# Head 0 of the first cross attention: keys loaded straight into the stacked layout and split there, the queries scaled tile by tile

## The reference

```python
q = qkv.reshape(bs * N_HEADS, ch, length)
k = v = y.reshape(bs * N_HEADS, ch, -1)
weight = jnp.einsum('bct,bcs->bts', q * scale, k * scale)
weight = jax.nn.softmax(weight.astype(jnp.float32), axis=-1)
a = jnp.einsum('bts,bcs->bct', weight, v)
...
x = x + _L0_xattn_ref(_layernorm(x, axis=-1), ctx_2048)
```

## Time and profile before

| what | value |
|---|---|
| median of 3 runs | 1378.21 us (1376.22 to 1380.72) |
| time of the profiled execution | 1381.22 us |
| its span | 1379.4 us |
| PE busy | 1337.7 us, 97% |
| DVE busy | 1098.2 us, 80% |
| ACT busy | 970.9 us, 70% |
| POOL busy | 156.3 us, 11% |
| DMA | 199.51 MB, mean 145 GB/s |

### The profile page before, as it was taken

One profiled execution on the slowest core, in us unless ns is written; L12 is line 12 of the kernel. 1 busy time (PEld: TensorE's weight loads), 2 busy tenths in 40 slices (PEclk: granted clock), 3 DMA queues, 4 the chain that ended last, 5 costly groups with the idle time before them and its releaser, 6 DMA issues. The chain is left out here.

```text
span 1379.4 us, 28331 instructions
## 1 busy us (share of the span) xinstructions
PE 1337.7 (97%) x10623; PEld 883.2 (64%) x10623; DVE 1098.2 (80%) x2195; ACT 970.9 (70%) x1892; POOL 156.3 (11%) x216
## 2 busy tenths in 40 slices
PE   3999999999999999999999999999999999999999
PEld 2544444444444444444457999999988874668998
DVE  5889989899999999997876766666668759887665
ACT  1499999999999999999574555555544631785553
POOL 4122221122222222112000000000000000000000
PEclk9899999999999999999999999999999999999999
DMA  7555566565665555555303755555529614204651
GB/s 189 124 143 116 126 173 166 154 164 110 142 143 127 115 135 131 121 96 79 100 1 139 305 184 186 184 187 186 190 94 373 244 68 177 69 1 129 183 190 39
DMA packets 75338, 199.51 MB, mean 145 GB/s; under 512 B 35512, under 2 KB 43616, under 8 KB 63040
## 3 DMA queue, kind: packets, MB, share of 16 engines
q1 hardware_dynamic: 75024, 197.69, 50.7%
q10 hardware_dynamic: 192, 0.20, 0.1%
HBM read 170.64 MB, written 23.80 MB: 141 GB/s over the span
## 5 line engine op out<-in xcount | busy, mean ns | idle before, releaser
L754 ACT ACTIVATE probs<-bank 128x512 f32<-128x512 f32 x1024 | 542.1, 619 | 54.3 <-PE bank L812 52.0
L672 DVE TENSOR_REDUCE pm<-bank 128x1 f32<-128x512 f32 x736 | 466.1, 682 | 51.2 <-PE bank L793 50.9
L812 PE MATMUL bank<-qst,kst 52*128 52x512 f32 (+1 forms) x1024 | 336.6, 437 | 7.8 <-DMA qst<-nscratch 7.1
L793 PE MATMUL bank<-kst,qst 48*128 48x512 f32 x904 | 315.6, 452 | 21.4 <-DMA qst<-qsplit 20.3
L824 PE MATMUL bank<-probs,vext 128*32 128x256 f32 (+3 forms) x4024 | 295.1, 394 | 0.8
L812 PEld LDWEIGHTS bank<-qst,kst 52*128 52x128 f32 (+1 forms) x1024 | 163.6, 187 | 197.3 <-DVE pm L672 93.6
L1602 PE MATMUL bank<-e_xhi,e_hi 128*128 128x256 f32 (+1 forms) x768 | 217.6, 283 | 0.3 <-DVE e_xlo L283 0.2
L1602 PE MATMUL bank<-e_xhi,e_lo 128*128 128x256 f32 (+1 forms) x768 | 217.5, 283 | 0.0
L1602 PE MATMUL bank<-e_xlo,e_hi 128*128 128x256 f32 (+1 forms) x768 | 217.5, 283 | 0.0
L824 PEld LDWEIGHTS bank<-probs,vext 128*32 128x32 f32 x4024 | 92.6, 109 | 117.8 <-issue 103.9
L793 PEld LDWEIGHTS bank<-kst,qst 48*128 48x128 f32 x904 | 140.5, 189 | 30.5 <-DMA qst<-qsplit 20.3
(11 more groups left out here) (251 smaller groups left out, 1763.8 us busy)
## 6 DMA issues: line engine op xcount, KB each, us to landing
raw<-wall SPq DMA_DIRECT2D x43, 1536.0 KB, 6.6
kst<-kscratch SPq DMA_DIRECT2D x192, 128.0 KB, 4.4
kscratch<-ksplit SPq DMA_DIRECT2D x15, 1024.0 KB, 4.3
kraw<-ctx_rows SPq DMA_DIRECT2D x16, 512.0 KB, 6.2
vraw<-ctx_vt SPq DMA_DIRECT2D x16, 512.0 KB, 6.3
ctxT<-ctxT SPq DMA_DIRECT2D x8, 1024.0 KB, 9.7
nat<-ctx_chunks SPq DMA_DIRECT2D x6, 1024.0 KB, 19.9
weights<-wscratch SPq DMA_DIRECT2D x16, 256.0 KB, 3.8
```

Source lines behind the costliest of these rows:

```text
L672: nc.vector.tensor_reduce(max_at(p, 1), bank[:, pre_bank(p), :], AX.X, ALU.max).then_inc(pre_reduced, 1)
L754: nc.scalar.activation(probs[:, (XST * k + n) % PR, :], bank[:, score_bank(XST * k + n), :], ACT.Exp, scale=XSCALE).then_inc(probs_ready, 1)
L793: ins = nc.tensor.matmul(bank[:, pre_bank(p), :], qst[64 * j:64 * j + KR, h, tt * P:tt * P + P], keys, start=True, stop=True)
L812: nc.tensor.matmul(bank[:, score_bank(s), :], kst[64 * j:64 * j + rows, h % 2, m * P:m * P + P], qst[64 * j:64 * j + rows, h, :], start=Tr ...
```

## The change

Head 0's keys are no longer rounded, stored and loaded again. SP loads them raw, straight into the stacked layout: `load_first(half)` issues eight transfers of 16 partitions x 2048 numbers, the four groups of 16 rows in both partition halves, into `first_raw`. A column `low_row` holds 1 on the rows of the low part and 0 elsewhere. One multiplication writes `first_high` (rounded keys on the low rows, zero elsewhere) and one subtraction writes `kst`: key minus rounded key on the low rows, the rounded key on the others. DVE does this for the first half, POOL for the second (`second_keys`). The second half's loads wait for the first half's and for the queries in `qst`.

The token tiles are loaded and normalised apart: tile 0 first, on DVE; tile 1's statistics follow on DVE behind the keys, and its scaling and splitting go to POOL (`second_queries`). The memsets of `marks` go to the front of POOL's list, and POOL now runs `second_keys()`, `split(1)`, `split_apart(1)`, `second_queries()` in this order. `load_q` waits for its own tile only. The loads of head 1's raw keys and pairs stand behind `load_first(1)`.

```diff
+FIRST_LOADS = 8 * 16
+FIRST_KEYS = [1, 3]
+SECOND_SCALED = 14
...
+            def load_first(half):
+
+                keys = ctx_rows[0].rearrange("(c s) n -> c (s n)", c=XC)
+                for row in range(0, 64, XC):
+                    for j in range(2):
+                        lo = j * XK + half * XK // 2
+                        sp.dma_start(first_raw[64 * j + row:64 * j + row + XC, half, :], keys[:, lo:lo + XK // 2]).then_inc(kraw_loaded[0], 16)
+
-            sp.dma_start(X[:, :, :], x.rearrange("(a p) d -> p a d", p=P)).then_inc(x_loaded, 16)
-            load_raw(0)
+            sp.dma_start(X[:, 0, :], x[0:P]).then_inc(x_loaded[0], 16)
+            load_first(0)
+            sp.dma_start(X[:, 1, :], x[P:]).then_inc(x_loaded[1], 16)
+            sp.wait_ge(kraw_loaded[0], FIRST_LOADS)
+            sp.wait_ge(stack_lo[0], 96)
+            load_first(1)
             load_raw(1)
             load_pairs(1)
-            sp.wait_ge(split_step, 1)
-            sp.dma_start(kscratch[0, 0], ksplit[:, 0, :].bitcast(F32)).then_inc(first_high_stored, 16)
-            sp.wait_ge(split_step, 2)
-            sp.dma_start(kscratch[0, 1], ksplit[:, 1, :].bitcast(F32)).then_inc(split_stored, 16)
-            sp.wait_ge(first_high_stored, 16)
-            load_rows(0, 0, K_ROWS[0])
-            load_rows(0, 0, K_ROWS[2])
-            sp.wait_ge(split_stored, 16)
-            load_rows(0, 0, K_ROWS[1])
-            sp.wait_ge(stack_lo[0], 192)
-            load_stack(0, 1)
-            sp.wait_ge(qsplit_ready, 4)
...
+            def second_keys():
+
+                pool.wait_ge(kraw_loaded[0], FIRST_LOADS * 2)
+                pool.wait_ge(split_step, FIRST_KEYS[0])
+                nc.gpsimd.tensor_scalar(first_high[:, 1, :], first_raw[:, 1, :], low_row[:, :], None, ALU.mult).then_inc(split_step, 1)
+                pool.wait_ge(split_step, FIRST_KEYS[0] + 1)
+                nc.gpsimd.tensor_tensor(kst[:, 0, XK // 2:], first_raw[:, 1, :], first_high[:, 1, :].bitcast(F32),
+                                        ALU.subtract).then_inc(split_step, 1)
...
+            second_keys()
+            split(1)
+            split_apart(1)
+            second_queries()
...
+            dve.wait_ge(kraw_loaded[0], FIRST_LOADS)
+            link(nc.vector.tensor_scalar(first_high[:, 0, :], first_raw[:, 0, :], low_row[:, :], None, ALU.mult))
+            nc.vector.tensor_tensor(kst[:, 0, 0:XK // 2], first_raw[:, 0, :], first_high[:, 0, :].bitcast(F32),
+                                    ALU.subtract).then_inc(split_step, 1)
+            dve.wait_ge(x_loaded[1], 16)
+            tile_spread(g, 0, 1, link)
+            tile_small(g, dve, 0, 1, link)
...
-                    pe.wait_ge([stack_lo, stack_hi][half][h % 2], stacked(h, half))
+                    if h == 0:
+                        pe.wait_ge(split_step, FIRST_KEYS[half])
+                    if k != 1:
+                        pe.wait_ge([stack_lo, stack_hi][half][h % 2], stacked(h, half))
```

More of the change, by code:

```diff
@@ L88, in raw_loads @@
 def raw_loads(h):
[L89 removed]
+    return 80 * (h // 2 + h % 2) + FIRST_LOADS * NS * (1 - h % 2)
 def cuts(h):
[L93 removed]
+    return 5 * h
 def stacked(h, half):
[L97 removed]
+    return [192, 96][half] * (h // 2 + 1) + 48 * (h // 2 + h % 2) - 96 * (1 - h % 2)
 def score_bank(s):
@@ L189, in setup @@
     return g
[L193 to L215, removed]
 def roots(k, a):
-    return TA * k + a
+    return TA * k + a + 1
 def turned_bank(k, a):
@@ L436, in load_stack @@
                 if half == 0:
-                    sp.wait_ge(split_stored, 32 * h + 16)
+                    sp.wait_ge(split_stored, 32 * h)
                 if h >= 2:
@@ L587, in values @@
                 nc.gpsimd.tensor_copy(vext[:, h % 2, :, 0:XC], vraw[:, h % 2]).then_inc(v_ready, 1)
-            split(0)
-            pool.wait_ge(qsplit_ready, 4)
-            split(1)
-            split_apart(1)
+            def second_keys():
[5 more added lines that the diff above has]
+                                        ALU.subtract).then_inc(split_step, 1)
             nc.gpsimd.memset(marks[:, :, :].bitcast(F32), 1.0).then_inc(const_set, 1)
@@ L631, in _ @@
                 if h == XH - 1:
-                    pool.wait_ge(split_stored, 32 * XH - 16)
+                    pool.wait_ge(split_stored, 32 * (XH - 1))
                     pool.wait_ge(nsplit_step, 2 * NS * h + 2)
@@ L649, in link @@
                 dve.wait_ge(dve_step.sem, dve_step.inc(ins))
-            dve.wait_ge(x_loaded, 16)
-            norm_dve(g, dve, link)
-            for a in range(TA):
-                dve.wait_ge(g.xn_ready, a + 1)
-                nc.vector.tensor_copy(qsplit[:, 0, a], xn[:, a, :]).then_inc(qsplit_ready, 1)
-                dve.wait_ge(qsplit_ready, 2 * a + 1)
-                nc.vector.tensor_tensor(qsplit[:, 1, a], xn[:, a, :], qsplit[:, 0, a].bitcast(F32), ALU.subtract).then_inc(qsplit_ready, 1)
+            dve.wait_ge(g.ident_ready, 2)
+            link(nc.vector.tensor_reduce(low_row[:, :], ident[:, :].rearrange("p (j r c) -> p r j c", j=2, c=XC)[:, 1], AX.XY, ALU.add))
+            dve.wait_ge(x_loaded[0], 16)
+            tile_spread(g, 0, 0, link)
+            tile_scale(g, dve, 0, 0, link)
+            dve.wait_ge(g.xn_ready, 1)
+            nc.vector.tensor_copy(qsplit[:, 0, 0], xn[:, 0, :]).then_inc(qsplit_ready, 1)
+            dve.wait_ge(qsplit_ready, 1)
+            nc.vector.tensor_tensor(qsplit[:, 1, 0], xn[:, 0, :], qsplit[:, 0, 0].bitcast(F32), ALU.subtract).then_inc(qsplit_ready, 1)
+            dve.wait_ge(kraw_loaded[0], FIRST_LOADS)
[5 more added lines that the diff above has]
+            tile_small(g, dve, 0, 1, link)
+            link(nc.vector.scalar_tensor_tensor(out=g.rstd[:, 1, :], in0=g.std[:, 1, :], scalar=1.5, in1=g.rstd[:, 1, :],
+                                                op0=ALU.add, op1=ALU.mult))
             def turn_negmax(k):
@@ L739, in _ @@
             nc.scalar.activation(g.warm[:, :], ident[:, 0:1], ACT.Sqrt)
-            act.wait_ge(kraw_loaded[0], 16)
-            nc.scalar.copy(ksplit[:, 0, :], kraw[:, 0, :]).then_inc(split_step, 1)
-            act.wait_ge(g.var_ready, 1)
-            nc.scalar.activation(g.std[:, :, :], g.var[:, :, :], ACT.Sqrt).then_inc(g.std_ready, 1)
+            tile_root(g, act, 0, 0)
             for row, part in Q_ROWS:
```

31 lines of the change are left out of this document (23 added, 8 removed).

## The result

| | before | after |
|---|---|---|
| median | 1378.18 us (4 runs, 1376.22 to 1380.72) | 1391.88 us (4 runs, 1391.21 to 1392.72) |
| profiled execution and its span | 1381.22, 1379.4 us | 1391.84, 1390.0 us |

The ratio is 1.0091, with a 95% interval of 1.0070 to 1.0111: the change makes the kernel slower by 13.7 us on the medians. The whole interval lies outside the 0.3% that count as no change. Three of 21 later executions of the kernel before took 1385.5 to 1387.6 us, so medians are compared here and not single executions.

What follows compares the result with a forecast made beforehand. The first real score, held by SP's queue behind POOL's split of head 1, bounds the start: 33.1 + 5.7 + 12.5 = 51.3, score 4.9 later at 56.2, +8.4 us; 1378.2 + 8.4 = 1386.6 us, range 1379.0 to 1393.6.

Steps and rivals of the forecast that it cites:

- Only the start counts, and the first score carries it: Whole kernel: PE is busy after the start, so the change is worth the first real score's shift, 47.77 to 56.2 us.
- PE's start: First pre product at 15.5 us: direct loads landed at 12.0, then DVE's multiplication 1.2 and subtraction 2.3; first pair 17.8.
- The rival of slower loads: Direct loads of head 0's keys at 117 GB/s, 2.1 us more per half: +4.2, 1390.8 us; chance 0.12.
- The head start is eaten by the queue: First pair 3.4 us earlier, but SP's queue delays the score; the rival that it reaches the end: 1374.8 us, chance 0.09.
- POOL's multiplication, 1.9 us between 1.8 and 4.7: POOL multiplies 2048 columns of head 0's second half: 1.9 us, sized from a memset, a copy and a two-input instruction.
- Head 1's keys stored at 33.1: SP's store of head 1's keys at 33.1 us instead of 23.05, since POOL's split(1) stands behind head 0's second half.
- 5.7 us from the store to the key loads: SP's queue from the store of head 1's keys to the key loads, marks included: 5.7 us, before 7.27.
- 12.5 us from the key loads to the store of the maxima: SP's queue from first key load to the store of the maxima: 12.5 us carried over, so stored at 51.3.
- The queue would not stall on the marks (0.18): Rival on SP's queue: key loads take 2.7 us, the score comes at 50.2, +2.4, 1380.6 us; chance 0.18.
- The clock, no term: PE's low clock after restart loses 3.7 us as before, so no term; twice as long, 1390.3 us, had chance 0.06.
- DVE idle until about 41.5 for POOL's split maxima: DVE waits for POOL's split_negmax(0) until about 41.5 us; its seven pairs end at 50, before the score, so free.
- The score ended by the maxima's loads: Sign in the profile: the first score near 56 us, its wait ended by the maxima loaded into qst.

Runs made afterwards that it cites:

- e1: Changed kernel with the multiplication of the second half of head 0's keys moved from POOL to ACT: 1388.12 us, ratio 1.0065.
- e4: Changed kernel with head 1's raw keys and pairs loaded, and POOL's split of head 1 run, ahead of head 0's second half: 1389.51 us, ratio 1.0077.
- e5: Changed kernel with two of the four copies of marks, those for head 1's buffer, issued on ACT's queue: 1389.89 us, ratio 1.0087.
- e8: Changed kernel with the edits of e4 and e1, POOL's second_keys behind queries and memsets, and marks behind head 1's stacked-key and query loads: 1379.81 us, ratio 1.0010.
- e9: As e8, with the two copies of marks for head 1's buffer on ACT's queue behind its multiplication: 1380.58 us, ratio 1.0017.
- e10: As e8, with only head 0's two copies of marks ahead of the first maxima and head 1's two behind the first score's inputs: 1375.28 us, ratio 0.9983.
- e11: Changed kernel with only head 1's two copies of marks moved behind the first score's inputs: 1386.75 us, ratio 1.0070.
- e2: Kernel before, with SP holding the store of head 1's keys until 13 pairs of pre tiles are reduced: 1391.92 us, ratio 1.0095.
- e3: Changed kernel with PE's first pre product held until the second half of head 0's raw keys has landed: 1394.11 us, ratio 1.0111.
- e12: Kernel before, with head 1's two copies of marks moved behind the first score's inputs: 1378.33 us, ratio 0.9992.
- e7: Changed kernel with 30 more filling products on PE behind the last pre product: 1389.22 us, ratio 1.0084.
- e6: Changed kernel with POOL's multiplication by the constant 1.0 instead of low_row, which makes the second half's keys wrong: 1392.04 us, one run.

## Why the prediction was right, and where not

The forecast was 1386.6 us in 1379.0 to 1393.6, slower with a chance of 0.73. The kernel is slower, at 1391.88; the median lies in the range, 5.3 us above the forecast. By its steps:

- **Only the start counts, and the first score carries it.** Right. The shift of the score and of the median against before are +13.4 and +13.7 us; in e1 +10.0 and +9.9, in e4 +10.0 and +11.3, in e5 +12.4 and +11.7, in e8 +2.7 and +1.6, in e9 +2.4 and +2.4, in e10 -1.8 and -2.9, in e11 +9.7 and +8.6, in e2 +13.3 and +13.7, in e3 +14.7 and +15.9, in e12 -0.9 and +0.2. They agree within 1.4 us. e7 is the exception (+14.8 and +11.0), with its shorter stretch of low clock.
- **PE's start.** 15.5 predicted, 14.58 measured, just below the 15 to 16.5 that were to show it; first pair 17.8 and 16.59. The eight direct loads were issued from 1.20 and had landed at 10.92. The sum let them start at 4.1 and take 6.9 us at 152 GB/s; they had landed 6.8 us after 4.1, and from 4.1 to 10.9 the engines moved 164 GB/s, token tile 1 and the queries included. The second half landed 9.4 us after its first issue, where the sum has 9.2 (of these, 1.4 and 0.9 us stand there without a row). The rival of slower loads fell. The Trainium skill, page "SBUF — State Buffer", section "Door 1: The DMA port swizzle", gives 104 GB/s for a transfer to 16 partitions at 1 MiB; with several such transfers in flight, to different rows, the engines moved about half more here.
- **The head start is eaten by the queue.** Right. It is now 4.6 us and changes nothing of the score; e3 gave up 8.1 us of it and lost 2.2 at most.
- **POOL's multiplication, 1.9 us between 1.8 and 4.7.** Wrong: 5.45 us, above the upper bound. This is the first failed step, +3.55 us. I had put it beside a memset and a copy because it has one input; the rows say that it costs more than the subtraction of the same size with two inputs (4.62, predicted 4.6). The Trainium skill, page "GPSIMD Engine Reference", section "Engine selection", calls operations with one input roughly line-rate; the trace agrees for the copy of 1024 in 1.04 us, 1.0 ns for a column, and disagrees for TENSOR_SCALAR, 2.7 ns for a column.
- **Head 1's keys stored at 33.1.** 35.95: 3.55 late by the multiplication, 0.8 early by the landing at 22.3 instead of 23.1.
- **5.7 us from the store to the key loads.** Wrong: 9.1 us (35.95 to 45.04), 3.4 more, of which the marks are 3.0: the four took 5.96 us to issue and not 2.99. This is the second failed step; I had carried the row over as it stood, though I took the marks to be slow. Before, the queue took all four, and the hold fell on a key load behind them (a single issue of 4.12 us); now it falls on the third and the fourth mark already, and the key loads are the shorter for it: 7.51 instead of 8.75. Why the queue took four at once before, and only two here, is not shown.
- **12.5 us from the key loads to the store of the maxima.** 11.3. In sum -1.2 us. Together: 3.55 - 0.8 + 3.4 - 1.2 = 4.95, which is 61.15 - 56.2.
- **The queue would not stall on the marks (0.18).** It fell. In e8 six key loads with no marks ahead of them took 2.63 us to issue; behind two marks on another queue, in e9, 7.16.
- **The clock, no term.** Only in the net. The stretch at the low level was 17 us and not 10, nearly the twice that was given 0.06. Against the kernel before, the changed one was 1.6 us behind for a while and 0.5 later, not 3.7; against e7, with 10 us of it, 2.6 us.
- **DVE idle until about 41.5 for POOL's split maxima.** It was 45.18, by the late multiplication and by `second_queries`, 4.1 us instead of 2.5 with the scaling alone at 2.08, and free as said: 56.34 is 11 us later.
- **The score ended by the maxima's loads.** The profile names none ("issue", 8.38 us idle), so this part of the test could not be read. The score runs 1.45 us after the last of these loads was issued (59.70), and in e10, where they are named, 1.39 us after (44.60).
- **The range.** The chain, from POOL's split of head 1 through SP's queue to the first score, was right, and so was the direction. That the time lies in the range is in part luck. The upper end, 1393.6, is made of the slower loads (4.2) and the multiplication at its upper bound (2.8). The loads were not slower; without their 4.2 us the range would have ended at 1389.4, below what was measured. What filled that room is a multiplication beyond its bound and 3.0 us of marks that stood in no bound.

## What to carry to other kernels

Follow the event that the steady part waits for, not the one that the change moves forward: here PE started 5.8 us earlier, and the first score ran 13.4 us later, because the split that feeds a queue in order had been put behind new work on the engine that is slowest at it. Before lifting one gate in such a queue, look for the next (e4 got back 2.4 us of 13.7; with the second gate and the slow transfers moved too, e10 came out 16.6 us ahead of the change). And place transfers like these marks, 64 KB into 4 partitions each, behind what is urgent: on another queue they delayed the urgent ones just the same (e5, e9).

## What the runs showed of the hardware

- POOL's TENSOR_SCALAR from 2048 f32 columns to fp32r took 5.45 us, 5.39 with a constant, while a cast of 1024 took 1.04 and a subtraction of 2048 took 4.62. DVE did the same multiplication in 1.29 us and ACT in 2.00.
- Four copies of 64 KB into 4 partitions each took 2.99 to 6.61 us to issue, by the kernel. Two alone took 1.34 to 1.77 us wherever they stood, and the transfers behind them paid then: six query loads took 6.63 us in e10 against 3.78 in e8, and six key loads 6.13 in e11 and 4.12 in e12 against 2.63 in e8 (8.75 behind four marks). This holds across the two issuing queues (e5, e9). One held issue took the same time whatever the transfer was: the fourth mark in the changed kernel, the second key load in e11, the second query load in e10:

```profile
42.48 2.52 SPq L491 DMA_DIRECT2D kst<-marks  x1
```

```profile
43.41 2.52 SPq L418 DMA_DIRECT2D kst<-kscratch  x1
```

```profile
35.48 2.52 SPq L457 DMA_DIRECT2D qst<-qsplit  x1
```

  No run varied the shape of the marks, so whether it is their few partitions or the 16 KB in each of them is open.
- In e8 the loads of the maxima waited until 47.61 though the data engines were nearly idle by 44 (columns as in the earlier trace rows):

```profile
44.00:47.00 3.00, 0.36 (x4) 0.00 (x0) 2.50 (x3) 0.00 (x0) 0.00 (x0) 0.82 0.02 4
```

The wait counts the marks as well as the store, so the late one may be either. Why its signal came some 3 us after the data is open.

- Start-up varies: the second half's loads, behind the same instructions, were issued at 12.91 us in the changed kernel, 13.80 in e7, 13.88 in e5, 14.13 in e3 and 14.38 in e6. Times of single profiled executions can't be compared more finely than these 1.5 us.
